# Graph attention and a Mamba-2 block on one core: transposes in pairs, edge codes one block later, and a clamp on GpSimd in place of VectorE

## The chip, the cores and the metric

The kernel runs on one core of a Trainium2 chip. The metric is the device time of one execution in microseconds; three executions of the kernel before the change took 786.87, 787.05 and 788.37 us, so the median is 787.05 us. The engines are TensorE (PE, with its weight loads shown as PEld), VectorE (DVE), ScalarE (ACT), GpSimd (POOL) and SyncE (SP), which issues the DMAs.

## The reference

There are 4096 nodes with 128 features each, and a dense 4096 x 4096 adjacency matrix `adj` of zeros and ones in fp32 (64 MB). The first layer is a graph attention whose matrix is used twice:

```
x   = layernorm(x)
e   = leaky_relu(x @ a1 + (x @ a2).T, 0.2)
U   = softmax(where(adj > 0, e, -9e15), axis=1)
rowsum = sum(U * 0.5 * U, axis=1)
feat = c2 * (U@x - x*rowsum) + (1 - c2) * (x + U@x - x*rowsum)
feat = sign(feat) * max(|feat| - 1e-6, 0)          # soft threshold
out  = mix of feat, U@feat, rowsum, h0             # second product with U
```

`c0` to `c4` are sigmoids of `temp`. The second layer is a Mamba-2 block over the 4096 rows as one sequence in 32 chunks of 128 (input projection, a convolution of four taps, a state recurrence over chunks, gating, norm, two output projections). Both layers are added to their input.

## The kernel before

**The trick with the attention.** Since leaky_relu has two slopes, exp(e) is a product of a row factor and a column factor on either side of zero. So each edge is only put into one of two classes, A (slope 1) or C (slope 0.2). A code byte per edge says which class it is in, or that there is no edge. Two 0/1 mask matrices, `maskA` and `maskC`, are made from the codes. `Y` holds the features times the column factors, in a high and a low part. TensorE multiplies masks by `Y`, and the row factors are applied afterwards.

**Tiling of round 1.** The 32 row tiles of 128 nodes are taken in 8 supertiles of 4 tiles (`NG` = 8, `IT` = 4). A supertile has 16 blocks b (`BLOCKS`). Block b does two things. First, `products` for row tile b // 4 against columns chunk b % 4: eight matmuls of 260 columns for A into `accA` (L1701), eight for C into `accC` (L1710). Second, for the *next* supertile, `turn(G + 1, b)`: four bf16 matmuls of 128 columns against the identity that transpose the 4 x 128 x 256 edges of block b into one of four PSUM banks `ps` (L1640, `TRB` = 4). After 4 blocks one row tile is complete.

**What the other engines do in block b.** Every engine has its own instruction list in a fixed order, written out by hand; they meet at semaphores.

- ACT: `sign(G + 1, b)` turns the fp32 adjacency that SP has loaded into bytes in `edges` (L1275), then `mask_a` makes `maskA` for block b + 2 (L1338, `LEAD` = 2, four buffers). At b % 4 == 1 it reads the accumulators of the tile before (L1361, L1362).
- DVE: `mask_c` makes `maskC` for block b + 2 (L785), then two `codes` instructions (L777) read the transposed edges of block b out of PSUM and write the codes of the next supertile. At b % 4 == 2 it adds `sum1` (L802, the sums of row tile T - 1, where T is the running tile) and `feat1` (L811, L812), which finishes the features of row tile T - 2: a clamp of `scaled` to +-1e-6 into `fwork`, and `scaled - fwork` into `xn`, which is the soft threshold.
- POOL: `features(T, k)` (L527 to L550), one call for each of the row tiles 0 to 29, two calls (k = 0 and 1) in a loop body: about sixteen small instructions, nearly all dependent on each other, from the sums of a row tile to `scaled`. It starts when `sum1` has counted up `summed`, and counts up `scaled_done`, for which `feat1` waits. For k = 1 it also adds two finished tiles into `featsum` (L555). One call is named a call below; its number is that of its row tile.
- SP: loads of `adj`, four in flight, each issued after a `sign`; and after blocks 5, 8, 11 and 14 the spill of a finished row of codes to DRAM, once `coded` is complete.

The helper `link` makes an instruction's successor wait for its end; `step` and `step_to` only count.

**Waits that the change bears on.** `turn` waits for `signed` of its block and for the codes four blocks before (`coded`). `codes` waits for `tr_done` of its transpose. `mask1` for block 3 of a supertile (made at b = 1) waits for all 32 `codes` of that supertile. `mask_a` and `mask_c` wait for `mm_done` of the product that last read their buffer.

**The last supertile and round 2.** In supertile 7 there are no turns and codes. In their place ACT (L1333) and DVE (`y2_low`, L764) make `Y2`, the scaled features for the second product, tile by tile as `feat1` finishes them. `feat1` runs here at b % 4 == 3, for row tiles 26, 27 and 28, and for 29 behind the supertile; row tiles 30 and 31 are finished on DVE alone (L919 to L946). Round 2 multiplies the same masks, made again from the codes, by `Y2`, and beside it runs the Mamba-2 block in 32 steps (from about 355 us to the end).

Of the kernel before, what the change touches and what calls it, by code (L numbers as in the profile page):

```python
# [25 lines left out]
ALU = mybir.AluOpType  # L26
# [5 lines left out]
THRESH = 1e-06  # L32
# [7 lines left out]
def gnn_ffn_kernel(nc, x, adj, h0, a, temp, W_in, conv_w, conv_b, dt_bias, A_log, D, norm_w, W_out, W_lin, b_lin, out):  # L40
    N, F = x.shape
    NT = N // P
# [4 lines left out]
    BLOCKS = IT * NB  # L47
    JH = NT // BLOCKS
# [14 lines left out]
    with ExitStack() as ctx:  # L63
# [62 lines left out]
        featw = sb("featw", [P, 2, F])  # L126
        scaled = sb("scaled", [P, 2, F])
        fwork = sb("fwork", [P, 2, F])
# [110 lines left out]
        S = {n: sem(n) for n in names}  # L239
# [202 lines left out]
        def _(pool):  # L442
            g = nc.gpsimd
            chain = [0]
# [77 lines left out]
            def features(T, k):  # L522
                row = g.snap(T) if not isinstance(T, int) else T
                n = {q: small[:, i:i + 1] for i, q in enumerate("E e r zn rho q qa rr s".split())}
                wait(pool, "summed", T + 1)
                pool.wait_ge(S["roww_done"], 2)
                step_to(g.tensor_copy(small[:, 0:2], roww[:, bass.ds(row, 1), :].rearrange("p a b -> p (a b)")))  # L527
                step_to(g.tensor_tensor(num[:], ps_sum[:, k, 0], ps_sum[:, k, 1], ALU.add))
                pool.wait_ge(S["pch"], chain[0] - 1)
                g.tensor_scalar(n["qa"], acc_q[:, k, 0:1], acc_q[:, k, 1:2], n["E"], ALU.add, ALU.mult).then_inc(S["taken"], 1)  # L530
                pool.wait_ge(S["pch"], chain[0])
                link(g.tensor_scalar(n["zn"], num[:, F:F + 1], 0.0, float(N), ALU.is_equal, ALU.mult))
                pool.wait_ge(S["taken"], T + 1)
                step_to(g.tensor_tensor(n["s"], num[:, F:F + 1], n["zn"], ALU.add))
                step_to(g.tensor_scalar(n["q"], num[:, F + 1:XC], n["e"], n["qa"], ALU.mult, ALU.add))
                pool.wait_ge(S["pch"], chain[0] - 1)
                link(g.tensor_tensor(n["r"], n["s"], consts[:, 1, 0:1], ALU.pow))
                step_to(g.tensor_tensor(featw[:, 0], col_mean[:], n["zn"].broadcast_to([P, F]), ALU.mult))
                link(g.tensor_scalar(n["rr"], n["r"], n["r"], 0.5, ALU.mult, ALU.mult))
                step_to(g.tensor_tensor(featw[:, 1], featw[:, 0], num[:, 0:F], ALU.add))  # L540
                link(g.tensor_scalar(n["rho"], n["q"], n["zn"], n["rr"], ALU.add, ALU.mult))

                wait(pool, "feat_done", T - 1)
                if k == 1 and (not isinstance(T, int) or T >= 3):
                    feature_sum(T - 3)
                step_to(g.tensor_tensor(k_one[:, k], coef[:, 5:6], n["rho"], ALU.subtract))
                link(g.tensor_tensor(featw[:, 1], featw[:, 1], n["r"].broadcast_to([P, F]), ALU.mult))
                link(g.tensor_tensor(featw[:, 0], xn[:, bass.ds(row, 1), :].rearrange("p a b -> p (a b)"), k_one[:, k].broadcast_to([P, F]), ALU.mult))
                g.tensor_tensor(scaled[:, k], featw[:, 0], featw[:, 1], ALU.add).then_inc(S["scaled_done"], 1)
                link(g.tensor_copy(row_out[:, bass.ds(row, 1), :].rearrange("p a b -> p (a b)"), small[:, 2:6]))  # L550
                end_chain()

# [150 lines left out]
        def _(dve):  # L703
# [68 lines left out]
            def codes(G, par, jt):  # L772

                n = G * NT + jt
                dve.wait_ge(S["tr_done"], n + 1)
                rows = bass.ds(v.snap(G * 512) if not isinstance(G, int) else G * 512, 512)
                v.scalar_tensor_tensor(  # L777
                    out=code[par][:, :, jt * P:(jt + 1) * P], in0=f1_rows[:, rows].rearrange("p (i r) -> p i r", i=IT),
                    scalar=neg_f2[:, jt:jt + 1], in1=turned(jt),
                    op0=ALU.is_le, op1=ALU.subtract).then_inc(S["coded"], 1)  # L780
# [23 lines left out]
            def feat1(T, k):  # L804

                row = v.snap(T) if not isinstance(T, int) else T
                mine = xn[:, bass.ds(row, 1), :].rearrange("p a b -> p (a b)")
                wait(dve, "feat_done", T)
                dve.wait_ge(S["scaled_done"], T + 1)
                inside = chain[0] > 0  # L810
                link(v.tensor_scalar(fwork[:, 1], scaled[:, k], -THRESH, THRESH, ALU.max, ALU.min))  # L811
                v.tensor_tensor(mine, scaled[:, k], fwork[:, 1], ALU.subtract).then_inc(S["feat_done"], 1)  # L812
                if inside:
                    dve.wait_ge(S["feat_done"], T + 1)
                else:
                    end_chain()

            def supertile(G, par, first=False, last=False):
                for b in range(BLOCKS):
                    it, ch = b // NB, b % NB  # L820
                    if not (last and b + LEAD >= BLOCKS):
                        mask1(G, par, b + LEAD)
                    if not last:
                        if b == 0:

                            wait(dve, "maskA_ready", G * BLOCKS)
                            wait(dve, "spilled", G * IT * 16)
                        if first and b == 0:
                            dve.wait_ge(S["f1_copied"], 8)
                            dve.wait_ge(S["yC_done"], NB)  # L830
                            dve.wait_ge(S["yA_done"], NB)
                        for j in range(JH):
                            codes(G + 1, 1 - par, b * JH + j)
                    if ch == 2 and not (first and it < 1):
                        sum1(G * IT + (it - 1), (it - 1) % 2)
                    if ch == 2 and not (first and it < 2):
                        feat1(G * IT + (it - 2), it % 2)
# [9 lines left out]
            def link(ins):  # L847

                dve.wait_ge(S["vch"], step(ins))

            def end_chain():
                if chain[0]:
                    dve.wait_ge(S["vch"], chain[0])
                    v.sem_clear(S["vch"])
                chain[0] = 0
# [29 lines left out]
            def mask2(n, k, j):  # L885

                b = j % NB
                if isinstance(n, int) and n < 2 * NB:

                    T, ch = FIRST[n]  # L890
                    dve.wait_ge(S[f"codes_in{T}"], 16)
                    mask_c(n + R1, code0[:, T, ch * JB * P:(ch + 1) * JB * P], b)
                    return
                dve.wait_ge(S[f"codes_in{k}"], code_count(n, k, b))
                mask_c(n + R1, code0[:, k, b * JB * P:(b + 1) * JB * P], b)

            G = NG - 1
            for b in range(BLOCKS):
                it, ch = b // NB, b % NB
                if b + LEAD < BLOCKS:  # L900
                    mask1(G, 1, b + LEAD)
                else:
                    mask2(b + LEAD - BLOCKS, 0, b + LEAD - BLOCKS)
                if ch == (1 if it == IT - 1 else 2):
                    sum1(G * IT + (it - 1), (it - 1) % 2)
                for t in Y2_AT[b]:
                    y2_low(t)
                if ch == NB - 1 and it < IT - 1:
                    feat1(G * IT + (it - 2), it % 2)
# [25 lines left out]
                step(v.scalar_tensor_tensor(out=both_T[:, i], in0=col_mean[:], scalar=zn_T[:, i:i + 1], in1=ps_sum[:, i, 0, 0:F], op0=ALU.mult, op1=ALU.add))  # L935
            link(v.tensor_scalar(k_T, rho_T, -1.0, coef[:, 5:6], ALU.mult, ALU.add))
            mask2(4, 1, 0)
            for i in range(2):
                made = step(v.tensor_scalar(fwork[:, i], xn[:, NT - 2 + i, :], k_T[:, i:i + 1], None, ALU.mult))
            y2_low(NT - 7)  # L940
# [690 lines left out]
        def _(pe):  # L1631
# [82 lines left out]
            def supertile(G, par, first=False, last=False):  # L1714
                for b in range(BLOCKS):
                    it, ch = b // NB, b % NB
                    if first and b < LEAD:
                        turn(G + 1, b)
                        continue
                    if first and b == NB:  # L1720

                        pe.wait_ge(S["colmean_done"], 1)
                        pe.wait_ge(S["roww_done"], 1)
                    if ch == 0 and not (first and it < 2):

                        free_acc(G * IT + (it - 2))
                    products(G * BLOCKS + b, it % 2, b, ch, XC, 1 if first and it == 0 else None)
                    if not last:
                        turn(G + 1, b)

            def free_acc(T):
# [257 lines left out]
```

## Time and profile before

| | |
|---|---|
| runs | 786.87, 787.05, 788.37 us |
| profiled execution | 786.87 us, span 785.1 us |
| granted TensorE clock, mean | 0.991 |
| PE busy | 741.4 us (94%) |
| DVE busy | 726.4 us (93%) |
| ACT busy | 671.1 us (85%) |
| POOL busy | 632.7 us (81%) |
| PE share of the chain that ended last | 73%, DVE 13%, POOL 7% |
| transposes L1640 | 512 matmuls |
| codes L777 | 256 instructions, 178.2 us |
| mask C L785 | 256 instructions, 206.1 us |

The span is the time from the first to the last instruction of the profiled execution; its own time is 1.8 us more. Matmuls are pipelined, so a busy PE overlaps with itself: its pace is read from the distance between the starts of like instructions, not from their durations. Round 1 in its steady form lies between about 65 and 305 us, the last supertile between 305 and 338 us.

### The profile page before, as it was taken

The page shows a single profiled execution, that of the slowest core. Times are in us where ns is not written, and L with a number is a line of the kernel's source. Part 1 is how long each engine was busy: PE and PEld are TensorE (multiplying, and loading weights), DVE is VectorE, ACT ScalarE, POOL GpSimd, SP SyncE. Part 2 cuts the span into 40 slices and gives each one's busy share as a digit, 9 for nine tenths or more (in the row PEclk, how much of TensorE's full clock was granted, in tenths as well). Part 3 has the DMA queues.
Part 4 walks back from the last instruction along what each step waited for, and adds up shares of the span by engine and source line. Part 5 has one row for each costly group of instructions (what it writes and reads, how often), then busy time and mean ns, then how long its engine had stood idle before and what let it go on. Part 6 is the DMA issues. An engine that isn't in the chain of part 4 may idle for free.

```text
span 785.1 us, 21076 instructions
## 1 busy us (share of the span) xinstructions
PE 741.4 (94%) x6049; PEld 708.5 (90%) x6049; DVE 726.4 (93%) x1898; ACT 671.1 (85%) x1428; POOL 632.7 (81%) x1215
## 2 busy tenths in 40 slices
PE   3689999999999999987899999999999999999987
PEld 1378999999999999977899999999999999999975
DVE  6999999999999999797999999999989899989986
ACT  5999898999899898955888888888889898989865
POOL 5583788888888888886888888888888888888863
PEclk9989999999999999999999999999999999999999
DMA  7689898989898986022221212121212121210000
GB/s 218 187 258 316 288 298 272 313 276 343 260 324 283 307 286 239 18 66 68 68 65 46 68 45 68 43 67 43 67 46 67 44 69 41 70 42 18 10 4 15
DMA packets 97961, 110.43 MB, mean 141 GB/s; under 512 B 6865, under 2 KB 89713, under 8 KB 97905
## 3 DMA queue, kind: packets, MB, share of 16 engines
q1 hardware_dynamic: 97906, 109.78, 43.3%
q8 instruction: 25, 0.41, 0.2%
q14 instruction: 30, 0.25, 0.1%
HBM read 90.87 MB, written 18.89 MB: 140 GB/s over the span
## 4 chain that ended last, share of the span: by engine, by line
PE 73%; DVE 13%; POOL 7%; issue 3%; ACT 2%; DMA 1%; POOLq 0%; DVEq 0%; ACTq 0%
PE accA L1701 26%; PE accC L1710 25%; DVE code L777 4%; PE ps L1640 3%; PE ps L1808 3%; PE ps L1792 3%; PE ps L1825 2%; DVE maskC L785 2%; PE ps L1806 2%; PE ps L1790 2%; PE ps L1810 2%; PE ps L1844 2%; PE ps L1817 1%; PE ps L1827 1%; DVE Y L756 1%
## 5 line engine op out<-in xcount | busy, mean ns | idle before, releaser
L1338 ACT ACTIVATE maskA<-code 128x1024 fp32r<-128x1024 int8 x256 | 269.2, 1053 | 20.7 <-DVE code L777 17.6
L1701 PE MATMUL accA<-Y,maskA 128*128 128x260 f32 (+1 forms) x1792 | 270.0, 293 | 1.7 <-issue 1.6
L1710 PE MATMUL accC<-Y,maskC 128*128 128x260 f32 (+1 forms) x1792 | 253.2, 284 | 4.3 <-DVE maskC L785 4.3
L1701 PEld LDWEIGHTS accA<-Y,maskA 128*128 128x128 f32 x1792 | 232.3, 191 | 4.6 <-issue 2.2
L1710 PEld LDWEIGHTS accC<-Y,maskC 128*128 128x128 f32 x1792 | 228.9, 189 | 5.6 <-DVE maskC L785 5.5
L785 DVE TENSOR_SCALAR maskC<-code 128x1024 fp32r<-128x1024 int8 x256 | 206.1, 806 | 0.1
L777 DVE SCALAR_TENSOR_TENSOR code<-f_rows,neg_f,ps 128x512 int8<-128x512 int8 (+1 forms) x256 | 178.2, 739 | 1.7 <-PE ps L1640 0.5
L1275 ACT ACTIVATE edges<-adj_in 128x1024 int8<-128x1024 f32 x128 | 135.3, 1059 | 2.0 <-DMA adj_in<-in_adj_dram 2.0
L638 POOL TENSOR_TENSOR room_r<-room,room_r 128x256 fp32r<-128x256 f32 x128 | 97.7, 791 | 2.5
L1063 DVE SCALAR_TENSOR_TENSOR room<-room 128x128 f32<-128x128 f32 x270 | 86.2, 340 | 0.0
L1640 PE MATMUL ps<-ident,edges 128*128 128x128 bf16 x512 | 51.2, 224 | 10.0 <-ACT edges L1275 10.0
L1640 PEld LDWEIGHTS ps<-ident,edges 128*128 128x128 bf16 x512 | 30.1, 99 | 20.0 <-ACT edges L1275 10.8
L1701 PE MATMUL accA<-Y_2a,maskA 128*128 128x256 f32 x256 | 38.1, 291 | 0.0
L527 POOL COPY small<-roww 128x2 f32 (+1 forms) x30 | 12.4, 414 | 31.4 <-DVE ps_sum L802 30.0
L1710 PE MATMUL accC<-Y_2b,maskC 128*128 128x256 f32 x256 | 36.0, 283 | 1.5 <-DVE maskC L785 1.5
L1465 ACT COPY room<-ps 128x260 f32<-128x260 f32 x30 | 11.3, 377 | 29.8 <-PE ps L1792 29.8
L1477 ACT ACTIVATE room<-ps,room 128x128 f32<-128x128 f32 x90 | 35.2, 474 | 0.0
L1808 PE MATMUL ps<-room 128*128 128x64 f32 x248 | 34.5, 262 | 0.0
L1710 PEld LDWEIGHTS accC<-Y_2b,maskC 128*128 128x128 f32 x256 | 32.9, 192 | 1.7 <-DVE maskC L785 1.7
L1539 ACT ACTIVATE room<-room 128x64 f32<-128x64 f32 x124 | 33.3, 341 | 0.0
L989 DVE SCALAR_TENSOR_TENSOR room<-accC,roww,acc_s 128x256 f32<-128x256 f32 x32 | 15.5, 485 | 18.8 <-ACT acc_s L1359 12.9
L1808 PEld LDWEIGHTS ps<-room 128*128 128x128 f32 x248 | 32.6, 192 | 0.0
(275 smaller groups left out, 1624.0 us busy)
## 6 DMA issues: line engine op xcount, KB each, us to landing
adj_in<-in_adj_dram SPq DMA_DIRECT2D x128, 512.0 KB, 5.0
edge_codes<-code SPq DMA_DIRECT2D x32, 512.0 KB, 5.6
code<-edge_codes SPq DMA_DIRECT2D x32, 512.0 KB, 3.3
xn<-in_x_dram SPq DMA_DIRECT2D x4, 512.0 KB, 5.7
room<-in_x_dram SPq DMA_DIRECT2D x32, 64.0 KB, 1.8
room<-in_L_gnn_h_dram SPq DMA_DIRECT2D x32, 64.0 KB, 2.0
out_dram<-room SPq DMA_DIRECT2D x32, 64.0 KB, 1.6
room<-in_L_ffn_W_in_dram SPq DMA_DIRECT2D x1, 192.0 KB, 2.5
```

What stands on the lines that cost most here:

```text
L638: m = g.tensor_tensor(dam.rearrange("p a h w -> p (a h) w")[:, at], upto.unsqueeze(1).broadcast_to([P, NH // 2, P]), da_parts.rearrange("p ...
L777: v.scalar_tensor_tensor(out=code[par][:, :, jt * P:(jt + 1) * P], in0=f1_rows[:, rows].rearrange("p (i r) -> p i r", i=IT), scalar=neg_f2 ...
L785: v.tensor_scalar(maskC[:, b % MASKS], src, 1.0 - LINK, None, ALU.is_equal).then_inc(S["maskC_ready"], 1)
L1063: ins = v.scalar_tensor_tensor(out=conv[:, cb], in0=hist[:, kc, cb, tap:tap + P], scalar=conv_wt[:, cb, tap:tap + 1], in1=conv[:, cb], op0 ...
L1275: s.activation(pair, adj_in[:, h % 4].rearrange("p i (e w) -> p i e w", e=JH), ACT.Relu, bias=FREE, scale=HUGE).then_inc(S["signed"], 1)
L1338: s.activation(maskA[:, b % MASKS], src, ACT.Relu, bias=1.0 - LINK, scale=-1.0).then_inc(S["maskA_ready"], 1)
L1477: m = s.activation(conv[:, cb], second[:, cb * P:(cb + 1) * P], ACT.Identity, bias=conv_bt[:, cb:cb + 1], scale=conv_wt[:, cb, TAPS - 1:TAPS])
L1539: last = s.activation(xdtd[:, h * HD:(h + 1) * HD], xdt[:, h * HD:(h + 1) * HD], ACT.Copy, scale=expD[:, h, P - 1:P])
L1640: m = t_.matmul(ps[b % TRB][:, it * P:(it + 1) * P], edges[:, b % EDGE_SLOTS, it], ident2[:], start=True, stop=True)
L1701: t_.matmul(accA[k][:, 0:2 * cols], maskA[:, b % MASKS, l * P:(l + 1) * P], y2_of(jt, 0) if cols == F else Y[:, jt, 0, :, 0:cols], start=j ...
L1710: m = t_.matmul(accC[k][:, 0:2 * cols], maskC[:, b % MASKS, l * P:(l + 1) * P], y2_of(jt, 1) if cols == F else Y[:, jt, 1, :, 0:cols], sta ...
L1808: t_.matmul(ps[0][:, h * HD:(h + 1) * HD], mix_of(c)[:, h], xdt[:, h * HD:(h + 1) * HD], start=False, stop=h == (kb + 1) * P // HD - 1)
```

## The change

The diff is whole. `turn` is issued for two blocks at a time, behind the products of the second one. On DVE the `codes` of block b move to block b + 1, so those of block 15 come in block 0 of the next supertile. In `features` POOL gets a wait behind `scaled` and one more instruction, the clamp, which writes one of two halves of `fwork`; DVE's `feat1` keeps only the subtraction. One wait is added at the end of round 1, in front of the writes of `fwork` for row tiles 30 and 31.

```diff
@@ features (GpSimd)
-                g.tensor_tensor(scaled[:, k], featw[:, 0], featw[:, 1], ALU.add).then_inc(S["scaled_done"], 1)
+                link(g.tensor_tensor(scaled[:, k], featw[:, 0], featw[:, 1], ALU.add))
+                g.tensor_scalar(fwork[:, k], scaled[:, k], -THRESH, THRESH, ALU.max, ALU.min).then_inc(S["scaled_done"], 1)
@@ feat1 (VectorE)
-                inside = chain[0] > 0
-                link(v.tensor_scalar(fwork[:, 1], scaled[:, k], -THRESH, THRESH, ALU.max, ALU.min))
-                v.tensor_tensor(mine, scaled[:, k], fwork[:, 1], ALU.subtract).then_inc(S["feat_done"], 1)
-                if inside:
-                    dve.wait_ge(S["feat_done"], T + 1)
-                else:
-                    end_chain()
+                v.tensor_tensor(mine, scaled[:, k], fwork[:, k], ALU.subtract).then_inc(S["feat_done"], 1)
@@ supertile (VectorE)
+                    if b == 0 and not first:
                         for j in range(JH):
-                            codes(G + 1, 1 - par, b * JH + j)
+                            codes(G, par, (BLOCKS - 1) * JH + j)
+                    if b > 0 and not last:
+                        for j in range(JH):
+                            codes(G + 1, 1 - par, (b - 1) * JH + j)
@@ last supertile (VectorE)
+                if b == 0:
+                    for j in range(JH):
+                        codes(G, 1, (BLOCKS - 1) * JH + j)
@@ end of round 1 (VectorE)
             mask2(4, 1, 0)
+            dve.wait_ge(S["feat_done"], NT - 2)
@@ supertile (TensorE)
                     if first and b < LEAD:
-                        turn(G + 1, b)
+                        if b % 2:
+                            turn(G + 1, b - 1)
+                            turn(G + 1, b)
                         continue
@@
-                    if not last:
+                    if not last and b % 2:
+                        turn(G + 1, b - 1)
                         turn(G + 1, b)
```

## Rows read from the trace of the kernel before

**Rows 1.** Busy time by stretch, steady part of round 1 (start:end, length, then engines).
```profile
100.00:200.00 100.00, 100.00 (x903) 97.32 (x902) 97.77 (x172) 92.79 (x113) 83.09 (x184) 1.00 0.92 301
200.00:300.00 100.00, 100.00 (x905) 97.47 (x904) 97.98 (x170) 93.03 (x116) 84.57 (x189) 1.00 0.87 289
```
**Rows 2.** Timeline of PE, round 1 with turns (start us, us, what).
```profile
152.06 0.40 PE L1640 MATMUL ps<-ident,edges 128*128 128x128 bf16 x4
152.26 1.20 PE L1701 MATMUL accA<-Y,maskA 128*128 128x260 f32 x8
...
154.26 0.40 PE L1640 MATMUL ps<-ident,edges 128*128 128x128 bf16 x4
```
**Rows 3.** Timeline of PE, last supertile, without turns.
```profile
307.27 1.12 PE L1701 MATMUL accA<-Y,maskA 128*128 128x260 f32 x8
...
309.18 0.40 PE L1701 MATMUL accA<-Y,maskA 128*128 128x260 f32 x2
```
**Rows 4.** Waits between 100 and 300 us (in total, times, longest).
```profile
POOL small L527 <- DVE ps_sum L802: 14.2, 23, 1.3
ACT maskA L1338 <- DVE code L777: 11.6, 5, 2.6
```
**Rows 5.** Timeline of POOL, call 9 with its ends.
```profile
154.47 0.19 POOL L527 COPY small<-roww 128x2 f32 x1 [0.48 <-DVE ps_sum L802]
...
155.13 0.77 POOL L530 TENSOR_SCALAR small<-acc_q,small 128x1 f32<-128x1 f32 x1
155.99 0.24 POOL L532 TENSOR_SCALAR small<-num 128x1 f32<-128x1 f32 x1
...
158.90 0.84 POOL L541 TENSOR_SCALAR small<-small 128x1 f32<-128x1 f32 x1
...
162.03 0.40 POOL L548 TENSOR_TENSOR featw<-xn,k_one 128x128 f32<-128x128 f32 x1 [0.18 <-POOL featw L547]
162.51 0.46 POOL L549 TENSOR_TENSOR scaled<-featw 128x128 f32<-128x128 f32 x1
162.91 0.19 POOL L550 COPY row_out<-small 128x4 f32 x1
163.73 0.68 POOL L527 COPY small<-roww 128x2 f32 x1 [0.63 <-DVE ps_sum L802]
```
**Rows 6.** Timeline of POOL, where call 11 begins.
```profile
172.26 0.18 POOL L527 COPY small<-roww 128x2 f32 x1 [0.62 <-DVE ps_sum L802]
```
**Rows 7.** Timeline of POOL, where call 27 begins.
```profile
315.26 0.19 POOL L527 COPY small<-roww 128x2 f32 x1 [0.39 <-POOL row_out L550]
```
**Rows 8.** Timeline of DVE round `feat1` of row tile 8, and the mask behind that of row tile 9.
```profile
153.81 0.48 DVE L802 SCALAR_TENSOR_TENSOR ps_sum<-accC,roww,acc_s 128x260 f32<-128x260 f32 x1
154.21 0.22 DVE L811 TENSOR_SCALAR fwork<-scaled 128x128 f32<-128x128 f32 x1
154.57 0.29 DVE L812 TENSOR_TENSOR xn<-scaled,fwork 128x128 f32 x1
154.80 0.89 DVE L785 TENSOR_SCALAR maskC<-code 128x1024 fp32r<-128x1024 int8 x1
...
163.68 0.69 DVE L785 TENSOR_SCALAR maskC<-code 128x1024 fp32r<-128x1024 int8 x1
```
**Rows 9.** Timeline of DVE, last supertile and behind it, the four `feat1`.
```profile
314.85 0.23 DVE L811 TENSOR_SCALAR fwork<-scaled 128x128 f32<-128x128 f32 x1 [0.49 <-POOL scaled L549]
...
324.81 0.23 DVE L811 TENSOR_SCALAR fwork<-scaled 128x128 f32<-128x128 f32 x1 [2.83 <-POOL scaled L549]
...
334.08 0.23 DVE L811 TENSOR_SCALAR fwork<-scaled 128x128 f32<-128x128 f32 x1 [2.14 <-POOL scaled L549]
...
346.27 0.47 DVE L811 TENSOR_SCALAR fwork<-scaled 128x128 f32<-128x128 f32 x1
```
**Rows 10.** Timeline of POOL, where calls 0 and 1 begin.
```profile
74.84 0.41 POOL L527 COPY small<-roww 128x2 f32<-128x2 f32 x1 [12.09 <-DVE ps_sum L802]
...
83.41 0.18 POOL L527 COPY small<-roww 128x2 f32<-128x2 f32 x1 [1.52 <-DVE ps_sum L802]
```

## The prediction

> **What bounds the kernel now.** I read the busy time by stretch first, for which engine has no air in the long steady part of round 1. Between 100 and 300 us PE is at 100%, DVE at 98%, ACT at 93%, and POOL only at 83 to 85% [rows 1]. PE overlaps with itself, so I took its pace from the timeline. A block with a turn takes 2.20 us from turn to turn [rows 2], a block without one 1.91 us [rows 3]; a turn costs 0.29 us. Its four matmuls explain less: the four are busy 0.40 us together, one lasts 0.22 us (L1640's mean on the page is 224 ns), so they start (0.40 - 0.22) / 3 = 0.06 us apart and are worth 0.24 us. The other 0.05 us is lost between the two kinds of matmul.
>
> POOL's 84% misleads. Its work is one chain of small dependent instructions, and the wait between two calls of `features` is all the air it has: 14.2 us over 23 calls, 0.62 us each, put down to `sum1` [rows 4]. Much of that is not air. Call 9 runs from 154.47 to 163.10 (162.91 + 0.19) and call 10 begins at 163.73 [rows 5]. The sum it waits for begins, by the distance 153.81 to 154.80 in rows 8, 0.99 us before the mask of 163.68, at 162.69, and ends at 163.17. So POOL had hardly to wait; the rest, 0.56 us, is the loop's branch. Call 11 begins at 172.26 after 0.62 us [rows 6]; where the sum is certainly there long before, POOL needs 0.39 us [rows 7]. So an odd call (9.26 us from start to start) has no air and an even one (8.53 us) 0.23 us; over the other even calls it is 0.1 to 0.23, and I take 0.2. Of the 17.79 us of a pair POOL needs 17.6. PE needs 8 blocks of 2.20, 17.65 with a few gaps. Three engines stand within 2% of each other, and POOL is the one to which the change adds.
>
> In the last supertile POOL is the bound outright: PE has no turns there (4 blocks are 7.65 us), `feat1` follows `feat1` after 9.96 and 9.27 us, and DVE stands waiting for `scaled` 0.49, 2.83 and 2.14 us [rows 9].
>
> **The change part by part.**
>
> *Turns in pairs.* 112 turns stood in 111 groups (the first two of supertile 0 already together) and stand in 56: 7 groups fewer in supertile 0, 8 in each of the six others, 55 in all. At 0.05 to 0.07 us (the upper end if the first matmul of products behind a turn hides less of its weight load than the row's mean says) that is 2.8 to 3.9 us of PE. A pair of row tiles needs 17.65 - 4 x 0.06 = 17.4 us on PE. It is worth something only as far as PE sets the pace.
>
> *Codes one block later.* DVE's work is the same. `codes` of an odd block, whose turn came with the pair, and of the even one before it are both there, so DVE never waits longer than before. Behind the wait of the first `codes` stand the masks for blocks that PE reaches two blocks later; nothing. The last codes of a supertile are complete one mask and two codes later, 0.6 + 1.3 = 2 us. `maskA` of block 3 waits for them; ACT already waits there 11.6 us in 5 times [rows 4]. PE needs that mask three blocks after the turn, 6.5 us, and it is made by 1.4 (codes now) + 2.0 + 1.1 (the mask) = 4.5 us, so 2 us of cover are left; ACT's idle 7% is 2.5 us in a supertile of 35 us, so it catches up. SP's spill of codes waits for the same count, and behind it stands a load of `adj`, which itself waits for a `sign` that comes later. I take 0; if the cover were gone the price is up to 1 us in each of 6 supertiles.
>
> *The clamp leaves DVE.* From clamp to subtraction 0.36 us in round 1 (154.21 to 154.57 [rows 8]), 30 times. DVE needs about 17.5 us a pair (98% of 17.79), then 16.8. As it is not the bound then, this is worth nothing by itself, except in the last supertile, where DVE picks up right behind `scaled`: 0.23 us for row tile 28 and 0.47 for 29 [rows 9], together 0.7, 0.8 us with the gaps behind them.
>
> *The clamp comes to POOL.* No row has this instruction on POOL. From below: a two-operation instruction on one column is 0.24 us (L532 [rows 5]). From above: two full inputs of 128 columns take 0.46 (L549). It reads one tensor, so I take the middle, 0.35 us. The wait: a dependent instruction starts 0.08 us behind the end (162.03 + 0.40 to 162.51), while an independent one starts 0.06 before it (162.51 + 0.46 to 162.91). So `row_out` starts 0.54 + 0.29 = 0.83 us behind `scaled`'s start in place of 0.40: 0.42 us more in each call, by the ends 0.31 to 0.53.
>
> The Trainium skill ("GPSIMD Engine Reference", Performance versus the Vector engine) gives about 1.03 cycles an element for one-input bodies, against 2.6 with two inputs; by this my value holds. The same section says that elementwise work is about twice as slow on GpSimd as on VectorE; twice the 0.22 us of L811 would be 0.43 us, and the sum below 2 us higher.
>
> *What POOL gets back.* The maskC instruction of DVE holds POOL up. In call 9 the first mask (154.80 to 155.69 [rows 8]) falls on L530, one column wide and 0.77 us long where the like L532 takes 0.24; L541 with 0.84 is another, and call 10 opens with an L527 of 0.68 for 0.19, beside the mask of 163.68 [rows 5, 8]. That is 0.5 us for each of the four masks of a tile. The skill (same page, Key points) names the cause: GpSimd shares its SBUF interfaces with VectorE, and two-port instructions contend; the trace agrees for masks. Now the mask after `feat1` moves. DVE's clamp began 0.12 us behind `scaled`'s end in call 9 (163.68 less the 0.59 from clamp to mask in rows 8, against 162.97); the subtraction will begin that long behind the clamp on POOL, and the mask 0.23 us later (154.57 to 154.80), so it runs from 0.35 to 1.04 us. POOL opens its next call at 0.52 (odd) or 0.76 us (even), so half of this mask falls where POOL stands anyway. It costs up to 0.28 us where it cost 0.5, and about 0.45 where it cost 0.55: 0.32 us back per pair. The other three masks of a tile fall elsewhere than now, each with 0.3 to 0.6 us; I take their cost unchanged.
>
> *The wait on `feat_done`* at the end of round 1: that count is complete since L812 of row tile 29, several instructions before. 0.
>
> **The sum.** Calls 0 to 2 have more air than 0.42 (1.52 us ahead of call 1 [rows 10]), so they only follow PE, which by then has saved 9 groups, 0.6 us. From call 3 to 25 POOL is the pace: 12 odd calls with 0.42 = 5.0, 11 even ones with 0.42 - 0.2 = 2.4, less 11.5 x 0.32 = 3.7 back, is 3.7; less the 0.6 is 3.1. Calls 26 to 28 each add 0.42, and one or two gaps give 0.3 back: 1.0. So `scaled` of row tile 28 comes 4.1 us later. DVE's chain of `y2_low` begins there and is busy until round 2, so all behind it moves, less 0.8: 3.3 us. Row tile 29's `scaled` was early by 2 us and stays so. From 786.87 us, the profiled execution (0.2 below the median), that gives 790.2 us.
>
> **Rivals.**
>
> 1. *POOL keeps up, PE sets the pace (faster).* Call 0 shows that phase matters: it took 83.41 - 1.52 - 74.84 = 7.05 us [rows 10] where call 10 took 172.26 - 0.62 - 163.73 = 7.91 with the same instructions [rows 5, 6]. If the masks in their new places take 0.5 us less per pair beyond the 0.32, POOL is at 17.6 and PE's saving begins to show; at 1 us less, 17.1, it shows wholly: -3.8 + 1.0 - 0.8, 783.3. Against it: three masks still fall into each call.
> 2. *It cancels.* Clamp at its lower end (0.31) and 0.2 more back per pair: 26 x 0.11 and 2.3 us off is 785.0; with half of it, 787.6. What POOL is late, PE's spare buffers and the smaller DVE load take up.
> 3. *POOL gets nothing back (slower).* The three other masks take what the first one gives: 3.7 + 0.3 more, 794.2; with the clamp at 0.53, 797. This decides as soon as a call costs POOL more than the 0.2 us of air it has, in the place of the forecast's own mechanism.
> 4. *The late codes starve ACT.* Above: up to 6 us more. Against it 2 us of cover.
>
> **How the numbers follow.** Forecast (POOL paces, 788.5 to 792.5) 0.33; rival 1 0.25; rival 2 0.22; rivals 3 and 4 0.20. A change under 0.2% (1.6 us) can't be told from none here. Faster 0.27, the same 0.23, slower 0.50. The range leaves out 2 in 10: the low end to 784.0, reaching most of rival 1, the high end to 795.0, the middle of rival 3; the likeliest case's own range is 788.5 to 792.5.
>
> **What would show it.** Right: in the profile after, starts of L527 some 18.1 us apart per pair between 110 and 300 us, all gaps of POOL at 0.39 or 0.63, the new clamp at 0.35 us, DVE idle ahead of L812 in round 1 with `scaled` or `fwork` as releaser, PE with gaps ahead of `maskC`, and DVE busy down from 98%. PE's turns stand eight together and a block pair without waits takes 4.34 us. Wrong: if the pairs are 17.4 us apart and DVE never waits for POOL in round 1, POOL's time was not as rigid as I say, and the contention with masks is the step that failed; if DVE is not late and PE gaps stand ahead of `maskA`, it is ACT. If the calls take 18.4 us a pair, nothing was given back.

## The result and the profile after

The changed kernel takes 796.01 us (median of 4 runs, 794.74 to 796.91) against 787.71 us (4 runs, 786.87 to 789.63): ratio 1.0101, 95% interval 1.0076 to 1.0125. It is 1% slower. The direction was forecast; the size, 8.3 us, is more than twice the 3.3 us forecast, and the time lies 1 us above the range.

These lines show the kernel after. The first is from section 4 of the page, the chain that ended last; the others are the busy time by stretch, with the columns of [rows 1].

```profile
PE 49%; POOL 32%; DVE 10%; issue 5%; ACT 2%; POOLq 1%; DMA 1%; DVEq 0%; ACTq 0%
```
```profile
100.00:200.00 100.00, 96.15 (x866) 93.52 (x865) 92.60 (x152) 89.88 (x111) 84.70 (x187) 1.00 0.89 291
200.00:300.00 100.00, 95.72 (x865) 92.90 (x864) 92.15 (x152) 86.02 (x108) 83.86 (x191) 1.00 0.84 276
```

POOL's share of that chain went from 7% to 32%. The busy time of PE and DVE fell by 4 to 6% per stretch, and POOL's busy share is what it was [rows 1]: here a chain of dependent instructions that sets the pace shows 84%, not 100%. The waits between 100 and 300 us (in total, times, longest) say who waits now. These are six of the view's lines:

```profile
ACT maskA L1341 <- DVE code L778: 23.7, 5, 5.3
DVE xn L811 <- POOL fwork L550: 14.7, 16, 1.6
POOL small L527 <- POOL row_out L551: 10.8, 21, 0.6
PE ps L1643 <- ACT edges L1278: 4.1, 5, 0.9
PE accA L1704 <- issue: 2.0, 4, 0.6
PE accA L1704 <- ACT maskA L1341: 1.1, 3, 0.6
```

In [rows 4] POOL's gaps ended with DVE's sum; now 21 of 22 end with POOL's own last instruction, so POOL hardly waits for anyone, and DVE waits 16 times for the clamp. PE is reached last: its waits stand ahead of the turns and of the products with `accA`, none ahead of `maskC`. The delay can be read from wait to wait: DVE waits for POOL, ACT for DVE's codes, PE for ACT. This is the end of call 10 on POOL's timeline, to be set beside [rows 5] and [rows 6]:

```profile
172.53 0.46 POOL L549 TENSOR_TENSOR scaled<-featw 128x128 f32<-128x128 f32 x1
173.07 0.65 POOL L550 TENSOR_SCALAR fwork<-scaled 128x128 f32<-128x128 f32 x1
173.79 0.19 POOL L551 COPY row_out<-small 128x4 f32 x1
174.36 0.52 POOL L527 COPY small<-roww 128x2 f32 x1 [0.39 <-POOL row_out L551]
```

The clamp lasts 0.65 us. From L549 to `row_out` it is 1.26 us where it was 0.40, so a call has 0.86 us more. This is DVE at row tile 9, to be set beside [rows 8]; it stands idle for 1.57 us ahead of the subtraction.

```profile
163.36 0.48 DVE L803 SCALAR_TENSOR_TENSOR ps_sum<-accC,roww,acc_s 128x260 f32<-128x260 f32 x1
165.41 0.29 DVE L811 TENSOR_TENSOR xn<-scaled,fwork 128x128 f32 x1 [1.57 <-POOL fwork L550]
165.62 0.69 DVE L786 TENSOR_SCALAR maskC<-code 128x1024 fp32r<-128x1024 int8 x1
```

This is PE, to be set beside [rows 2] and [rows 3]. One wait stands behind the turns, the rest is without a gap:

```profile
149.92 1.20 PE L1704 MATMUL accA<-Y,maskA 128*128 128x260 f32 x8
150.97 1.11 PE L1713 MATMUL accC<-Y,maskC 128*128 128x260 f32 x8
151.92 1.12 PE L1704 MATMUL accA<-Y,maskA 128*128 128x260 f32 x8
152.88 1.11 PE L1713 MATMUL accC<-Y,maskC 128*128 128x260 f32 x8
153.84 0.62 PE L1643 MATMUL ps<-ident,edges 128*128 128x128 bf16 x8
154.96 1.21 PE L1704 MATMUL accA<-Y,maskA 128*128 128x260 f32 x8 [0.50 <-issue]
```

**Where the 9.1 us of span went.** It is taken from the starts of L527 and from the subtraction of row tile 28 (334.34 us before, 343.23 after):

```profile
99.46 0.68 POOL L527 COPY small<-roww 128x2 f32 x1 [0.57 <-DVE ps_sum L803]
...
304.51 0.52 POOL L527 COPY small<-roww 128x2 f32 x1 [0.39 <-POOL row_out L551]
```

Those are the starts of calls 3 and 25: 11 pairs in 205.05 us, 18.64 us a pair; before it was 17.74 (101.26 to 296.44). Call 3 begins 1.8 us earlier than before, the 23 calls 3 to 25 take 10.5 us longer (call 26 begins at 314.36, before at 305.70), calls 26 to 28 up to the subtraction take 28.87 us against 28.64, and all behind it takes 451.0 against 450.8. The loss lies almost whole in the steady part of round 1.

### The profile page after: what moved, and what is told of

It is laid out like the page before. It is cut to its first block, busy times and chain, and to the rows that moved or that the text cites. A ratio compares the mean times of both kernels' runs of the same rounds, so it can differ in the third digit from the quotient of the medians.

```text
span 794.2 us, 21047 instructions
## 1 busy us (share of the span) xinstructions
PE 742.6 (93%) x6049; PEld 709.9 (89%) x6049; DVE 722.4 (91%) x1868; ACT 670.0 (84%) x1428; POOL 645.1 (81%) x1245
## 4 chain that ended last, share of the span: by engine, by line
PE 49%; POOL 32%; DVE 10%; issue 5%; ACT 2%; POOLq 1%; DMA 1%; DVEq 0%; ACTq 0%
PE accC L1713 14%; PE accA L1704 14%; DVE code L778 3%; PE ps L1814 3%; POOL small L535 3%; PE ps L1798 2%; POOL fwork L550 2%; POOL small L539 2%; PE ps L1831 2%; POOL small L537 2%; POOL featw L540 2%; PE ps L1812 2%; PE ps L1816 2%; POOL featsum L556 2%; PE ps L1850 2%
## 5 line engine op out<-in xcount | busy, mean ns | idle before, releaser
L1704 PE MATMUL accA<-Y,maskA 128*128 128x260 f32 (+1 forms) x1792 | 265.7, 291 | 7.3 <-issue 3.7
L1643 PE MATMUL ps<-ident,edges 128*128 128x128 bf16 x512 | 43.2, 225 | 14.0 <-ACT edges L1278 13.9
L1704 PEld LDWEIGHTS accA<-Y_2a,maskA 128*128 128x128 f32 x256 | 32.5, 190 | 0.0
```

The lines of the kernel that those rows point to most:

```text
L1643: m = t_.matmul(ps[b % TRB][:, it * P:(it + 1) * P], edges[:, b % EDGE_SLOTS, it], ident2[:], start=True, stop=True)
L1704: t_.matmul(accA[k][:, 0:2 * cols], maskA[:, b % MASKS, l * P:(l + 1) * P], y2_of(jt, 0) if cols == F else Y[:, jt, 0, :, 0:cols], start=j ...
```

## The experiments

Every run has its own comparison with the kernel before on the same chip (786.7 to 787.9 us). The edits are given against the changed kernel or the one before. "Pair" is the distance from the start of call 3 to that of call 25, divided by 11, as above, in the profiled execution; it does not hang on how round 1 started.

| kernel | clamp | codes | turns | sums | time us | ratio, interval | pair us |
|---|---|---|---|---|---|---|---|
| before | DVE | same block | single | POOL | 787 | | 17.74 |
| after | POOL | later | pairs | POOL | 796.01 | 1.0101 [1.0076, 1.0125] | 18.64 |
| e1 | DVE | later | pairs | POOL | 783.19 | 0.995 [0.9934, 0.9966] | 17.60 |
| e2 | POOL | same | single | POOL | 801.64 | 1.0189 [1.0171, 1.0207] | 18.86 |
| e3 | POOL | later | pairs | left out | 781.16 | 0.9925 [0.9908, 0.9941] | 17.57 |
| e4 | other forms | later | pairs | POOL | 791.35 | 1.0056 [1.0035, 1.0076] | 18.23 |
| e5 | DVE | later | single | POOL | 782.20 | 0.9924 [0.9908, 0.9941] | 17.60 |
| e6 | DVE | same | pairs | POOL | 843.18 | 1.0705 [1.0687, 1.0723] | 21.92 |
| e8 | DVE | later | pairs | PE | 786.55 | 0.9979 [0.9965, 0.9994] | 17.93 |
| e9 | POOL | later | pairs | PE | 780.47 | 0.9907 [0.9891, 0.9924] | 17.53 |
| e10 | POOL | later | single | PE | 781.81 | 0.9938 [0.9922, 0.9955] | 17.66 |
| e11 | cheap form | later | pairs | POOL | 788.27 | 1.0021 [1.0009, 1.0033] | 18.09 |
| e12 | shared | later | pairs | PE | 779.91 | 0.9909 [0.9893, 0.9926] | 17.43 |

**e1: the clamp back on VectorE.** Against the changed kernel:

```diff
-                link(g.tensor_tensor(scaled[:, k], ...))
-                g.tensor_scalar(fwork[:, k], scaled[:, k], -THRESH, THRESH, ALU.max, ALU.min).then_inc(S["scaled_done"], 1)
+                g.tensor_tensor(scaled[:, k], ...).then_inc(S["scaled_done"], 1)
+                (feat1 on VectorE as before the change)
```

> The changed kernel with the clamp left on VectorE as before: turns in pairs and codes one block later stay. Theory P (GpSimd's chain of calls is the pace, the clamp there costs 0.73 us a call): the pair of calls falls from 18.7 us to the 17.6 us GpSimd needs without it, the saving of the paired turns shows in part, 783 to 786 us, a little faster than before. Rival A (the late codes starve ScalarE, whose wait for codes grew from 2.3 to 4.7 us a supertile): most of the loss stays, 791 us or more. If neither part alone matters: 787.

783.19 us, 0.5% faster than before. The clamp's place is worth 1.5% between e1 and the changed kernel, all of the loss and more. The late codes do not starve ScalarE: between 100 and 300 us it waits 13.1 us for them here, against 11.6 before [rows 4].

**e2: the clamp moved alone.** The kernel before with the diff's two edits in `features` and `feat1`, and the added wait.

> The kernel before with nothing but the clamp moved to GpSimd. Theory P: the pace is the same chain of calls, so a pair again takes 18.5 to 18.9 us and the time is 795 to 798 us, all of the loss or a little more since the paired turns are missing. Rival A: without the late codes no more than 2 us are lost, 787 to 789 us.

801.64 us, beyond the 795 to 798 expected: the loss is there without the other two edits, and they take back some 6 us of it (5.6 by the two medians, 6.9 by the two ratios). Pair 18.86 us. What was not foreseen is that here `sum1` also comes too late for PE (between 100 and 300 us):

```profile
DVE xn L811 <- POOL fwork L550: 20.0, 21, 1.7
PE accA L1697 <- DVE ps_sum L803: 3.1, 4, 0.9
```

**e3: no feature sum in the calls.** It leaves out the sum of the features but for its last pairs of tiles.

```diff
-                if k == 1 and (not isinstance(T, int) or T >= 3):
-                    feature_sum(T - 3)
```

> The changed kernel without the additions of finished tiles into featsum inside the calls (L556; the sum of the features is left out but for its last two pairs of tiles). It takes some 1.3 us out of every second call. Theory P: the pair of calls goes from 18.7 to about 17.5 us, where PE's 17.4 takes over; with the two calls of the last supertile the time falls by 13 to 16 us to 780 to 783 us. Rival A: GpSimd's time is not the pace, under 3 us gained.

781.16 us, in the range expected, and 17.57 us a pair, 1.07 less. Taking 1.3 us out of every second call gives most of it back: POOL's chain was the pace. Its gaps still end with its own `row_out`, 22 times of 23.

**e4: two other forms of the instruction.** It leaves the clamp out or halves it.

```diff
-                g.tensor_scalar(fwork[:, k], scaled[:, k], -THRESH, THRESH, ALU.max, ALU.min)...
+                if k == 0: g.tensor_scalar(fwork[:, k], scaled[:, k], -THRESH, None, ALU.max)...
+                else:      g.tensor_scalar(fwork[:, k], scaled[:, k], 1e-9, 1e-9, ALU.mult, ALU.add)...
```

> The changed kernel with two other forms of the instruction on GpSimd: for even calls one operation (max alone), for odd calls two operations multiply and add (the clamp itself is so left out or halved). It measures why the clamp lasts 0.65 us where 0.35 was predicted. If a second operation costs by itself: even calls 0.35 to 0.45, odd calls 0.65 us. If max and min are the dear ones: even 0.5, odd 0.35. If any one-input instruction over 128 columns is dear: 0.65 both. The time falls by 26 times what the mean falls, so to 789 to 796 us.

These are durations on POOL (min/median/max in ns), the first line of each instruction's own view: L551 is max alone, L553 is multiply and add, and the third line is the clamp of the changed kernel, max and min.

```profile
L551 POOL TENSOR_SCALAR fwork<-scaled x15: 543/549/1063, 80.9 to 337.6; 128x128 f32<-128x128 f32 x15
```
```profile
L553 POOL TENSOR_SCALAR fwork<-scaled x15: 297/298/299, 89.5 to 348.7; 128x128 f32<-128x128 f32 x15
```
```profile
L550 POOL TENSOR_SCALAR fwork<-scaled x30: 649/652/1169, 80.9 to 353.7; 128x128 f32<-128x128 f32 x30
```

Two arithmetic operations take 0.30 us, max alone 0.55, max and min 0.65. It is max (or min) that is dear, neither a second operation as such nor the width. The pair fell by 0.41 us where the two instructions fell by 0.10 and 0.35.

**e5: codes later alone.** The kernel before with the diff's edits of `codes`.

> The kernel before with the codes one block later and nothing else. PE's work is unchanged (17.65 us a pair of row tiles), GpSimd's too (17.6). Theory P: 786 to 788 us, no change. Rival A (late codes starve ScalarE): 789 us or more, with PE waiting for maskA or for edges behind each supertile's start.

782.20 us, 0.76% faster: neither theory expected that. The traces show where it comes from. Before the change, `sum1` of row tile 0 starts on DVE at 74.12 us and PE, which needs the accumulator that it frees, goes on at 74.70:

```profile
74.12 0.48 DVE L802 SCALAR_TENSOR_TENSOR ps_sum<-accC,roww,acc_s 128x260 f32<-128x260 f32 x1
```
```profile
74.70 1.19 PE L1701 MATMUL accA<-Y,maskA 128*128 128x260 f32 x8 [0.86 <-issue]
```

With codes later it comes 1.35 us earlier. DVE waits for no transposes in either trace there; it has done seven masks since 60.6 us in both, but six pairs of `codes` in place of seven (1.32 us a pair) when `sum1` comes:

```profile
72.77 0.48 DVE L802 SCALAR_TENSOR_TENSOR ps_sum<-accC,roww,acc_s 128x260 f32<-128x260 f32 x1
```
```profile
73.62 1.20 PE L1708 MATMUL accA<-Y,maskA 128*128 128x260 f32 x8
```

PE's stalls at the start of a row tile are gone, 1 us here and 0.06 to 0.1 us at many of the others (between 100 and 300 us some of its blocks were 2.27 or 2.31 us long among others of 2.207; in e5 all are 2.20 or 2.21). The pair falls from 17.74 to 17.60 us. That the shorter queue ahead of `sum1` is also the cause at those others is argued from this, not shown one by one.

**e6: pairs alone.** The kernel before with the diff's edits of `turn`.

> The kernel before with the turns in pairs and nothing else: VectorE's codes of an even block stand ahead of the masks and now wait until the products of the block behind. Theory P: PE falls to 17.4 us a pair, GpSimd stays at 17.6 and VectorE's waits cost 0 to 0.2 us a pair: 784 to 787 us. If the codes must be moved for the pairs to work: 790 us or more, VectorE waiting for the transposes.

843.18 us, 7% slower, far beyond both. DVE waits 35.5 us for transposes between 100 and 300 us, where the kernel before waits 0.4. Behind that wait stand the masks and `sum1`, and behind `sum1` stands PE:

```profile
POOL small L527 <- DVE ps_sum L802: 61.7, 18, 5.6
DVE code L777 <- PE ps L1640: 35.5, 34, 3.3
ACT maskA L1338 <- PE accC L1710: 29.3, 26, 2.8
...
PE accA L1701 <- DVE ps_sum L802: 14.9, 8, 1.9
```

e1 differs from e6 in the place of the codes (and one added wait at the end of round 1) and takes 783.19 us: the late codes are what makes the pairs possible. I had counted only the masks that stand behind the waiting `codes` and found room for them; PE also stands behind `sum1` (14.9 us) and behind ACT's reading of the accumulators (10.6 us). TensorE's granted clock was 0.96 and 0.97 in these two stretches, where e1 shows 1.00; no run separates that part. As an estimate, 4% of PE's 83.8 us in 100 are 3.4 us of the 19 us that e6 loses there.

**e8: sums on PE, clamp on VectorE.** Against e1; the calls' `feature_sum` and the last one are gone:

```diff
+            def feature_part(q):
+                ...
+                pe.wait_ge(S["feat_done"], (q + 1) * 8)
+                for t in range(q * 8, (q + 1) * 8):
+                    t_.matmul(ps[3][:, 0:F], ones[:], xn[:, t, :], start=t == 0, stop=False)
+            # behind the products p = 0, 1, 2 of round 2; tiles 24 to 31 in feature_mean
```

> A candidate: paired turns and late codes, the clamp on VectorE, and the sum of the finished features taken from GpSimd (L555 and its wait, 1.3 us in every second call) and made at the start of round 2 by PE, 28 fp32 matmuls with the tile of ones more, 0.2 us each, in gaps of 6 us that PE has there. Theory P: GpSimd goes to 16.3 us a pair and is off the path; VectorE at 17.5 is next, so only 1 to 2 us there, and 2.7 us in the last supertile (calls 27 and 29): 778 to 781 us. If PE's gaps don't hide the sums: up to 5 us more, 783 to 786.

786.55 us: 5.5 us above the 778 to 781 expected, and above the 783 to 786 for sums that PE does not hide. POOL has air, 32.7 us of gaps where its own part is about 11 (as in e9), and yet the pair is 17.93 us, longer than in e1. DVE paces here: it is 98.3% busy and its view shows no wait between 100 and 300 us. That is so in e1 too, but the masks last 0.75 us on average where they last 0.71 in e1. Eight masks at 0.04 us are the 0.33 us of the pair. These are three masks of e8 and what POOL does beside them:

```profile
152.15 0.81 DVE L782 TENSOR_SCALAR maskC<-code 128x1024 fp32r<-128x1024 int8 x1
...
155.18 0.89 DVE L782 TENSOR_SCALAR maskC<-code 128x1024 fp32r<-128x1024 int8 x1
157.31 0.68 DVE L782 TENSOR_SCALAR maskC<-code 128x1024 fp32r<-128x1024 int8 x1
```
```profile
152.49 0.79 POOL L547 TENSOR_TENSOR scaled<-featw 128x128 f32<-128x128 f32 x1
...
154.98 0.54 POOL L528 TENSOR_TENSOR num<-ps_sum 128x130 f32<-128x130 f32 x1
...
157.17 0.85 POOL L537 TENSOR_TENSOR small<-small,consts 128x1 f32<-128x1 f32 x1
```

A mask that begins while POOL adds the sums of a row tile (L528, 130 columns from two inputs) lasts 0.89 us in place of 0.69; one that begins beside the one-column L537 lasts 0.68, and there POOL's instruction is the long one (0.85 us; in e1 it is 0.55 to 0.56 or 0.85 to 0.86). Between 100 and 300 us a mask begins within each of the 23 L528 of e8, and all 23 masks last 0.89 us; in e1 this is so for 11, again at 0.89 each. Outside L528, 20 masks of e8 take 0.73 to 0.82 us, and in e1 a single one is long (0.90). So it is POOL's phase against the masks that lengthens them. Why the phase settles there in e8 no run shows.

**e9: sums on PE, clamp on GpSimd.** The same edit on the changed kernel.

> The changed kernel (clamp on GpSimd) with the same sums on PE. GpSimd then needs 17.4 us a pair, VectorE 16.8, PE 17.4. Theory P: as the kernel without the sums (781.2 us) plus what PE's 28 matmuls don't hide: 781 to 784 us, 1 to 3 us slower than the candidate with the clamp on VectorE. If the clamp's place no longer matters once GpSimd has air: within 1 us of that candidate.

780.47 us, 0.9% faster than before, and 6 us better than e8, the opposite order of what was expected. With the sums gone the clamp belongs on POOL, for in e8 DVE was the pace. POOL is not free of it: 22 of its 23 gaps again end with its own `row_out`, now at 17.53 us a pair, next to PE's 17.4.

**e10: e9 with single turns.**

> The kernel with clamp on GpSimd, codes later and sums on PE (780.5 us), but with each turn behind its own products as before. There PE is next to the pace, so this weighs the pairs: PE 17.65 us a pair of row tiles in place of 17.4. If the pairs are worth 0.06 us a group: 1 to 3 us slower, 781.5 to 783.5. If they are worth nothing because VectorE or GpSimd holds the pace at 17.5: within 1 us.

781.81 us; the pair is 17.66 in place of 17.53. That is the pace of PE with single turns (8 blocks of 2.207 us, 17.66). The pairs are worth 0.13 us a pair of row tiles there, until POOL's chain takes over. By the times alone (0.9938 [0.9922, 0.9955] against 0.9907 [0.9891, 0.9924]) the two kernels are barely told apart. With e5 and e1 (both 17.60 us a pair) the pairs are worth nothing.

**e11: an operation as cheap as predicted.** It leaves out the threshold.

```diff
-                g.tensor_scalar(fwork[:, k], scaled[:, k], -THRESH, THRESH, ALU.max, ALU.min)...
+                g.tensor_scalar(fwork[:, k], scaled[:, k], 1e-9, 1e-9, ALU.mult, ALU.add)...
```

> The changed kernel with the GpSimd instruction in the clamp's place as multiply and add in place of max and min, in all calls; everything else is equal (the threshold is so left out). It lasts 0.30 us in place of 0.65. This is the price that the prediction took. Theory P: a pair of calls falls by 0.7 us to 17.9, the time by 26 x 0.35 = 9 us to 786 to 788.5. If the added wait and not the operation were the cost: 793 us or more.

788.27 us (10 runs, 786.49 to 790.88), in the range expected; the pair is 18.09 us, where 17.9 was expected. The view of the end of call 10:

```profile
170.75 0.46 POOL L549 TENSOR_TENSOR scaled<-featw 128x128 f32<-128x128 f32 x1
171.30 0.30 POOL L550 TENSOR_SCALAR fwork<-scaled 128x128 f32<-128x128 f32 x1
171.66 0.19 POOL L551 COPY row_out<-small 128x4 f32 x1
```

The prediction had 18.1 us a pair and 790.2 us for an instruction of 0.35 us. The added wait and instruction still add 0.51 us to a call here, and the time is 0.2% above the kernel before.

**e12: the clamp shared.** Against e9; calls 26 to 29 are taken out of the loop.

```diff
+                if clamp and k == 0:       # GpSimd, even row tiles up to 24
+                    link(m)
+                    m = g.tensor_scalar(fwork[:, k], scaled[:, k], -THRESH, THRESH, ALU.max, ALU.min)
...
+                if k == 1 or (isinstance(T, int) and T >= NT - 6):   # VectorE, the others
+                    link(v.tensor_scalar(fwork[:, k], scaled[:, k], -THRESH, THRESH, ALU.max, ALU.min))
```

> A candidate: pairs, codes later, sums on PE, and the clamp shared: on GpSimd for even row tiles up to 24, on VectorE for the odd ones and in the last supertile. GpSimd then needs 16.8 us a pair, VectorE 17.2, PE 17.4: the pace is PE's, 1 to 2 us better than 17.53, and 0.4 us for each of calls 26 to 28: 776.5 to 779 us. If VectorE's masks are held up by GpSimd as in the kernel with all clamps on VectorE (786.5): 781 us or more.

779.91 us: not told apart from e9 (0.9909 [0.9893, 0.9926] beside 0.9907 [0.9891, 0.9924]), and 1 us above what was expected. The pair is at 17.43, PE's pace with pairs (17.4), with PE at 100% and DVE at 99%:

```profile
100.00:200.00 100.00, 100.00 (x922) 98.71 (x921) 98.81 (x168) 94.08 (x116) 82.58 (x191) 1.00 0.93 302
```

Its profiled execution was its slowest, 781.71 us, and began call 3 2.2 us later than e9's; the last section tells where these went. e9 and e12 both beat the kernel before and the changed one.

## Why the prediction was wrong

- **POOL is the pace, though it looks 84% busy:** right. POOL's gaps end with its own `row_out`, DVE waits for the clamp, and e3 and e11 move the time when they take something out of POOL's chain. One sign failed: PE's gaps were to stand ahead of `maskC` and stand ahead of the turns and `accA`, where the delay comes over ACT.
- **"It reads one tensor, so I take the middle, 0.35 us":** this is the step that failed, the size of one term. The clamp on POOL takes 0.65 us, above even the upper bound of 0.46. The upper bound came from a row with arithmetic; the lower one, L532 of [rows 5], does compare, but on one column, where the difference does not show (0.24 us, beside 0.26 for the two multiplications of L539 in the kernel before). e11, with the instruction at 0.30 us, took 788.3 us; the same sum with 0.30 in place of 0.35 gives 788.9. The 0.35 us between the two instructions are 9 us in 26 calls, and the changed kernel is 7.7 us slower than e11. The Trainium skill ("GPSIMD Engine Reference", Performance versus the Vector engine) has about 1.03 cycles an element for one-input bodies. The trace agrees with one such value for all two-operation forms only as far as multiply and add go (0.30 us at 128 columns, 0.06 above L532 on one column); max and min take 0.35 us more on the same 128 columns. Twice VectorE's time, the other rule that the prediction took from the Trainium skill there, falls short too: 0.43 us against 0.65.
- **"0.42 us more in each call":** measured 0.86. Of the 0.44 missing 0.30 is the instruction, and the rest is `row_out`, which starts 0.07 us behind the clamp's end and not 0.06 ahead of it. In e11 a call has 0.51 us more.
- **"0.32 us back per pair":** too small, which hid part of the miss. 17.6 + 2 x 0.86 would be 19.3; measured 18.64, so 0.7 us come back, and 18.64 is by this 0.53 above what the prediction had. The prediction looked at the first mask of a tile and left the other three unchanged. They did not stay: between 100 and 300 us L530 went from 0.57 to 0.34 us on average and L541 from 0.59 to 0.34, while L535 went from 0.57 to 0.80. Odd calls went from 9.26 to 10.00 us on average, even ones from 8.48 to 8.64. The sign "18.4 us a pair, nothing given back" would have misled: it was 18.64 with 0.7 given back.
- **The start:** call 3 came 1.8 us earlier, not 0.6. Two thirds of that stand already at call 0 (73.59 us in place of 74.84; e5 alone 73.49, e2 alone 74.74) and are the late codes' effect on `sum1`, which the prediction put at nothing. "DVE's work is the same" is true; what I did not ask is what else stood behind `codes`.
- **The last supertile:** forecast 1.0 us up to `scaled` of row tile 28, less 0.8 for the clamps gone from DVE there and behind, 0.2 in all; measured 0.2 up to the subtraction and 0.2 behind it. The sum was near; its two parts were not tested apart.
- **Turns in pairs:** the price was right (two blocks take 4.35 us, from 69.17 to 73.52 by the starts of `accA` on PE; predicted 4.34), and so was the saying that it is worth something only as far as PE is the pace.
- **Luck:** with 0.30 us for the instruction the sum would have been right within 1 us, but by errors that offset each other: the wait behind the clamp was too small by 0.13 us a call, and what POOL gets back and the earlier start were too small as well, the start by 1.2 us.
- **Rival 3** had the right time (794.2, or 797 with the dearest clamp) by the wrong reason: POOL did get something back, but the instruction cost more. **Rival 4** fell as a cause of its own: ScalarE waits 23.7 us and no longer 11.6 [rows 4], yet e1 and e5, with the same late codes, are faster than before, and e2, without them, has 19.3 us of that wait. **Rival 2** fell with the clamp's size: it needed 0.31 us and 0.2 us more back per pair, and the clamp took 0.65 with 0.4 more back. **Rival 1**, PE as the pace at 17.4 us a pair, is what e12 comes to, with the sums off POOL and the clamp shared.

What stays open: why POOL and the masks settle in the phase they have in each kernel, and why max costs 0.25 us more than arithmetic on GpSimd.

## What to carry to other kernels

Ask of an engine with a long dependent chain not how busy it is but what ended its gaps; if the gaps are its own, an instruction added is paid for on every turn. Here 1.72 us added to a pair cost 0.90 us: the rest was the air of 0.1 to 0.2 us and what the masks, falling elsewhere, gave back. Before moving an operation to GpSimd, measure that operation at that width: there max and min take twice the time of multiply and add. And where an engine's order is fixed, list everything that stands behind an instruction and who waits for it: moving `codes` one block later was the one edit of the three that made this kernel faster, and without it the pairs cost 7%.

## What the runs showed of the hardware

On GpSimd, 128 x 128 fp32 `tensor_scalar`: multiply and add 0.30 us (e4, e11), max 0.55 (e4), max and min 0.65 (changed kernel). On VectorE max and min take 0.22 us (kernel before).

A `maskC` instruction of VectorE lasts 0.69 us, and 0.89 when it begins within GpSimd's L528, 128 x 130 from two inputs (23 of 23 in e8, 11 of 11 in e1); one-column instructions of GpSimd that fall beside a mask last 0.77 to 0.86 us in place of 0.33 to 0.56 (L530 and L537: e8 has only the long ones, e1 both).

The granted clock of TensorE in the start of round 1 differs between executions. PE waits there for `edges`, until about 53 to 54 us. From 54 to 58 us the clock was then 1.00 (the level of 2.4 GHz) in the kernel before, the changed one, e2, e4, e5, e6, e9, e10 and e11, whose waits were 0.5 to 1.5 us. It was 0.57 in e1 (wait 1.50 us), 0.61 in e8 (1.93), 0.57 in e12 (2.46) and 0.51 in e3 (2.59), so mostly at the level of 1.2 GHz. The wait alone does not decide it: e1 and e9 waited equally long. The stretch of 46 to 62 us (column PEclk, third from the right) in e9 and then in e12:

```profile
46.00:62.00 16.00, 14.44 (x128) 13.88 (x126) 16.00 (x23) 13.86 (x18) 12.95 (x10) 0.95 0.83 258
```
```profile
46.00:62.00 16.00, 13.54 (x106) 13.10 (x104) 14.43 (x19) 13.42 (x18) 11.94 (x8) 0.84 0.80 241
```

In e12 the wait for `edges` ends 1.0 us later than in e9, and the sixteen matmuls with ones that follow are busy 3.38 us, at a granted clock of 0.54, where e9's take 2.05 at 1.00: these two make the 2.2 us that e12 is late at call 3. In e3 the same happened in the profiled execution (784.63 us; the three others took 780.85 to 781.40). The runs of one kernel spread by 0.7 us (e5, e10) to 4.4 us (e11). That the start makes most of this is argued, not shown, since one execution of each kernel was profiled. It is why the pairs above were compared by the distance of calls.
